# Cross-attention and FFN on one core: FFN products as 7 block products of half the size, and a new path for weights and products

## The reference

```python
x = x + attention(layernorm(x), ctx, ctx, Wq, Wk, Wv, Wo)      # 32 heads, 8 key/value heads
xn = layernorm(x)                                              # 1792 x 1024
g = xn @ (w1 * w1_scale).T                                     # w1: 3584 x 1024, one scale per 128x128 block
u = xn @ (w3 * w3_scale).T
h = silu(g) * u                                                # 1792 x 3584
out = x + h @ (w2 * w2_scale).T                                # w2: 1024 x 3584
```

## Time and profile before

| what | us |
|---|---|
| median of 3 runs | 2817.81 (2813.53 to 3363.06) |
| span of the profiled execution | 2817.7 |
| up to the end of attention | 897.8 |
| first output projection and norm | 897.8 to 997.0 |
| FFN, first half (with transposes) | 997.0 to 1890.5 |
| rest of it, second output projection | 1890.5 to 1996.5 |
| FFN, second half | 1996.5 to 2817.7 |

### The profile page before, as it was taken

How to read it: one execution, slowest core, us unless ns; L and a number is a source line. 1 busy time by engine, 2 the same in 40 slices (tenths; PEclk the granted TensorE clock), 3 DMA queues, 4 the chain that set the end, 5 groups by cost and what they waited for, 6 DMA issues and landing times. The chain is left out here.

```text
span 2817.7 us, 39477 instructions
## 1 busy us (share of the span) xinstructions
PE 2730.8 (97%) x14320; PEld 2311.9 (82%) x14320; DVE 1277.8 (45%) x2198; ACT 790.0 (28%) x1452; POOL 476.3 (17%) x221
## 2 busy tenths in 40 slices
PE   7989999999997999999999999999999999999999
PEld 6978777777763788888888888887888888888888
DVE  6425776777674533333333333335443333433343
ACT  3222444444444132222222222212211111112110
POOL 1000444444454121121111111100000000000000
PEclk9989999999986999999999999999999999999999
DMA  7525555454452332323222222243111111111101
GB/s 213 162 83 160 126 130 143 130 126 129 123 114 79 115 135 98 120 97 107 100 89 97 97 89 89 97 134 120 60 60 60 45 60 45 60 60 45 59 30 53
DMA packets 184786, 277.32 MB, mean 98 GB/s; under 512 B 62368, under 2 KB 140576, under 8 KB 184720
## 3 DMA queue, kind: packets, MB, share of 16 engines
q1 hardware_dynamic: 184720, 276.43, 32.0%
HBM read 190.20 MB, written 85.72 MB: 98 GB/s over the span
## 5 line engine op out<-in xcount | busy, mean ns | idle before, releaser
L74 PE MATMUL bank<-x_h,f_w_h 128*128 128x448 f32 x1792 | 667.3, 372 | 3.1 <-DVE f_w_l L80 3.1
L76 PE MATMUL bank<-x_h,f_w_l 128*128 128x448 f32 x1792 | 657.7, 367 | 0.0
L75 PE MATMUL bank<-x_l,f_w_h 128*128 128x448 f32 x1792 | 657.5, 367 | 0.0
L74 PEld LDWEIGHTS bank<-x_h,f_w_h 128*128 128x128 f32 x1792 | 337.6, 188 | 31.7 <-DVE f_w_l L80 3.5
L76 PEld LDWEIGHTS bank<-x_h,f_w_l 128*128 128x128 f32 x1792 | 337.3, 188 | 29.6
L75 PEld LDWEIGHTS bank<-x_l,f_w_h 128*128 128x128 f32 x1792 | 337.8, 189 | 28.4
L1341 DVE TENSOR_TENSOR f_hf<-bank,f_gate 128x448 f32<-128x448 f32 x112 | 69.6, 622 | 603.1 <-PE bank L76 524.8
L1353 DVE TENSOR_TENSOR y<-bank,y 128x512 f32<-128x512 f32 x392 | 270.1, 689 | 150.9 <-PE bank L76 148.2
L691 DVE TENSOR_REDUCE a_nm<-bank 112x1 f32<-112x375 f32 x512 | 268.1, 535 | 144.2 <-PE bank L826 141.5
L74 PE MATMUL bank<-f_w_h,f_h_h 128*128 128x512 f32 x784 | 312.4, 398 | 0.0
L76 PE MATMUL bank<-f_w_h,f_h_l 128*128 128x512 f32 x784 | 306.4, 391 | 0.0
(11 more groups left out here) (105 smaller groups left out, 3991.2 us busy)
## 6 DMA issues: line engine op xcount, KB each, us to landing
stash<-in_L_ffn_w SPq DMA_DIRECT2D x84, 512.0 KB, 4.6
weight_scratch<-f_wt SPq DMA_DIRECT2D x84, 512.0 KB, 2.7
stash<-weight_scratch SPq DMA_DIRECT2D x84, 512.0 KB, 4.0
stash<-in_ctx SPq DMA_DIRECT2D x48, 500.0 KB
a_qst<-q_scratch SPq DMA_DIRECT2D x96, 224.0 KB, 4.8
a_kst<-k_scratch SPq DMA_DIRECT2D x96, 188.0 KB, 4.2
stash<-in_L_xattn_Wo SPq DMA_DIRECT2D x64, 128.0 KB, 4.1
q_xn<-in_x SPq DMA_DIRECT2D x16, 448.0 KB, 6.0
```

What stands on the lines that cost most here:

```text
L74: pe.matmul(acc, lh, rh, start=first, stop=False)
L75: pe.matmul(acc, lh, rl, start=False, stop=False)
L76: return pe.matmul(acc, ll, rh, start=False, stop=last)
```

## The change

**Output projection.** `mixing()` runs once over all 14 tiles. Each tile with its residual goes to DRAM (`y_scratch`). The normalised tile is written with its columns in another order (32 columns of each of four quarters side by side) and transposed by PE; ACT alone copies the result, to `xT` for the first 7 tiles, and through `x_scratch` for the last 7. At its end SP waits for these stores.

**Gate and up products** (`gate_up`). The 1,792 tokens are two passes of 896 (g = 0, 1). A pass goes over 28 units `mi` (14 pairs of row chunks P, first w1 and then w3, m = 0 and 1). A unit is a 256x1024 block of weights by 1024x896 of tokens, as 2x2 blocks by 2x2 blocks in the Strassen-Winograd form: 7 block products i = 0 to 6, each 4 weight tiles (128x128) by 448 columns, 12 matmuls, 84 in a unit (before: 96). Their weight operands are three of the quarters and four sums S of them (POOL, `sums`), the token operands three blocks and four sums T. The products add up in three PSUM banks per parity of `mi` and in three tiles `su` on DVE (`add`, 5 per unit). h is stored to DRAM, as 3 blocks and 4 sums (POOL, `hidden_sums`), for the later down projection.

**Weights.** ACT multiplies the raw weights by their scales (`scale_raw`), DVE transposes them in blocks of 32x32 (`make_wT`, 4 passes per unit), SP stores them for the second pass (1 MB) and loads the raw weights of the unit after (1 MB, four DMAs to 32 partitions each, runs of 1 KB), into one buffer. In the second pass the transposed weights are read back, and the same is done with w2: `load_raw2` (1 MB, four DMAs to 32 partitions, runs of 256 bytes), `scale_raw2` (ACT, 8 passes of 128x256), `make_w2T` (DVE, 4 passes), `down_sums` (POOL, 4 passes), `store_w2`.

**Down projection** (`down`). After both passes, 7 block products of 896 x 1792 by 1792 x 512, each 7 tiles of 128 tokens, each 14 x 3 = 42 matmuls of 512 columns (49 x 42 = 2,058; before 2,352). Its operands are loaded from DRAM and split again. The residual (7.3 MB) is loaded at its start.

The PE transposes of weights are gone. The number of DMAs to 32 partitions and the waits that stand between them are new.

```diff
@@ gate_up, SP @@
+                        for mi in range(2 * NM):
+                            if mi == 2:
...
+                                sp.dma_start(xT[:, :, :], x_scr).then_inc(x_loaded_, 16)
+                            if mi >= NM + 2 and mi % 2 == 0:
+                                store_w2((mi - NM) // 2 - 1)
+                            if NM <= mi + 2 < 2 * NM:
+                                load_wT(mi + 2)
+                            if mi >= 2 and mi % 2 == 0:
+                                store_h(mi // 2 - 1)
+                            if mi + 2 < NM:
+                                store_wT(mi + 2)
+                                if mi + 3 < NM:
+                                    load_raw(sp, mi + 3)
+                            if mi >= NM and mi % 2 == 0:
+                                load_raw2((mi - NM) // 2)
+                        def store_wT(mi):
+                            sp.wait_ge(wT_made, 4 * mi + 4)
+                            sp.dma_start(wt_scr[mi], wT[:, mi % 2]).then_inc(wT_stored[mi % 2], 16)
+                        def store_h(P_):
...
+                            sp.wait_ge(h_done, 4 * P_ + 4)
+                            for i, b in ((0, H11), (2, H21), (5, H22)):
...
+                            for k, i in enumerate((4, 1, 3, 6)):
+                                sp.wait_ge(Sh_made, 4 * P_ + k + 1)
...
@@ gate_up, POOL: sums (S), hidden_sums, down_sums are 4 tensor_tensor each @@
+                        def sums(mi):
...
+                            wait_wT(pool, mi)
+                            wait(pool, w_lo, 7 * (mi - 1) + 5)
+                            pool.tensor_tensor(s1, a21, a22, ALU.add).then_inc(S_made, 1)
...
+                            wait(pool, w_lo, 7 * (mi - 1) + 7)
+                            pool.wait_ge(S_made, 4 * mi + 2)
+                            pool.tensor_tensor(s4, a12, s2, ALU.subtract).then_inc(S_made, 1)
+                        for mi in range(2 * NM):
+                            if mi >= 2 and mi % 2 == 0:
+                                hidden_sums(mi // 2 - 1)
...
+                            if mi + 2 < 2 * NM:
+                                sums(mi + 2)
+                            if mi > NM and mi % 2 == 1:
+                                down_sums((mi - NM) // 2)
@@ gate_up, ACT @@
+                        def first_copy(mi):
+                            P_ = mi // 2
+                            act.wait_ge(prod, 7 * mi + 1)
...
+                            nc.scalar.activation(su[:, 0, :], A_[mi % 2][:, 0:TB], ACT.Copy
+                                                 ).then_inc(first_out, 1)
+                            for i in range(7):
+                                act.wait_ge(prod, 7 * mi + i + 1)
+                                if i == 0:
+                                    first_copy(mi)
...
+                                        gate(P_, H11, A_[0][:, 0:TB])
+                                if mi == NM - 1:
+                                    split_x(1, i)
+                                if nxt:
+                                    split_w(mi + 1, i)
+                                if mi % 2 == 0:
+                                    if i in (4, 5, 6):
+                                        act.wait_ge(summed, 5 * mi + i - 1)
+                                        gate(P_, {4: H22, 5: H21, 6: H12}[i],
+                                             su[:, {4: 2, 5: 0, 6: 1}[i], :])
+                                if i == 1 and mi + 2 < NM:
+                                    scale_raw(mi + 2)
+                                if i == 3 and mi >= NM and mi % 2 == 0:
+                                    scale_raw2((mi - NM) // 2)
@@ gate_up, DVE @@
+                            for i in range(7):
+                                dve.wait_ge(prod, 7 * mi + i + 1)
+                                if i == 1:
...
+                                    add(mi, 1, B_, 0)
+                                elif i == 3:
+                                    add(mi, 2, B_, 0)
...
+                                if nxt:
+                                    split_w(mi + 1, i)
+                                if up and i >= 4:
...
+                                    hidden(P_, b, su[:, slot, :], i - 2)
+                                if 2 <= i <= 5 and mi + 2 < NM:
+                                    make_wT(mi + 2, i - 2)
+                                if i < 4 and mi >= NM and up:
+                                    make_w2T((mi - NM) // 2, i)
@@ gate_up, PE @@
+                                pe.wait_ge(w_lo, 7 * mi + i + 1)
...
+                                elif i == 2:
+                                    pe.wait_ge(first_out, mi + 1)
+                                elif i == 3:
+                                    pe.wait_ge(summed, 5 * mi + 1)
...
+                                elif i == 5:
+                                    pe.wait_ge(summed, 5 * mi + 2)
+                                elif i == 6:
+                                    pe.wait_ge(summed, 5 * mi + 3)
@@ down, SP @@
+                        sp.wait_ge(b_stored, 112 * NP)
+                        load_b(0, 0)
...
+                        load_a(0)
...
+                        load_b(0, 1)
+                        load_a(1)
...
+                        for t in range(MT):
+                            for r in range(2):
+                                for at, n, tok in rows(r, t):
+                                    sp.dma_start(y[at:at + n, r, t, :], y_scr[tok:tok + n, :]
+                                                 ).then_inc(y_loaded, 16)
...
+                        for n in range(N):
+                            i, t = n // MT, n % MT
+                            if n + 2 < N:
+                                load_a(n + 2)
```

More of the change, by code:

```diff
@@ L148, in load13 @@
[L148 to L162, removed]
-                src = wt_scr[bass.ds(2 * p + par, 1), 2].rearrange("a p n -> (a p) n")
-            sp.dma_start(dst, src).then_inc(r2_loaded[half][par], 16)
@@ L981, in _ @@
+                        store_xT(NT_TOK - 1)
+                        for s in range(2):
+                            sp.wait_ge(res_stored[s], 16 * NT_TOK // 2)
+                            sp.wait_ge(xT_stored[s], 16 * ((MT + s) // 2))
                     @block.gpsimd
                     def _(pool):
[L983 to L987 removed]
@@ L1114, in _ @@
                                     last.then_inc(o_done, 1)
-                        def step(t, slot, use):
-                            products(t, slot)
-                            transposes(t - 1, 1 - slot)
-                        tiles(pe, step)
-                        transposes(TT - 1, 0)
-        def ffn(half, y, x2_h, x2_l):
+                        for t in range(1, NT_TOK):
+                            products(t)
+                            transposes(t - 1)
+                        transposes(NT_TOK - 1)
@@ L1441, in pair @@
-                        def pair(p, more):
-                            for par in range(2):
-                                for tb in range(2):
-                                    gate_up(p, par, tb, more)
-                            pe.wait_ge(t_lo, t2_first(p, 1) + T2)
-                            for t in range(TT):
-                                down(p, t)
-                                if more and t < T13 and half == 0:
-                                    transpose13(p + 1, 1, t)
@@ L1458, in build_program @@
         queries()
         attention()
-        y = top.enter_context(nc.sbuf_tensor("y", [P, TT, D], f32))
-        x2_h = top.enter_context(nc.sbuf_tensor("x2_h", [P, KT, HALF], f32r))
-        x2_l = top.enter_context(nc.sbuf_tensor("x2_l", [P, KT, HALF], f32r))
-        for half in range(2):
-            mixing(half, y, x2_h, x2_l)
-            ffn(half, y, x2_h, x2_l)
+        with nc.sbuf_tensor("xT", [P, KT, HALF], f32) as xT:
+            mixing(xT)
+            gate_up(xT)
+        down()
```

1013 lines of the change are left out of this document (612 added, 401 removed).

## The result

The changed kernel takes 2944.66 us (median of 4 runs, 2941.84 to 2947.65). The kernel before took 2817.89 us beside it, so the ratio is 1.0456, with a 95% interval of 1.0441 to 1.0472: slower. (One of the four runs of the kernel before took 3363.06 us, in a slow state, and is left out of the ratio.) Forecast were 2859 us, 1.5% slower, and a difference that can't be told from none was the likeliest case. The time lies in the range, but the loss of 127 us is three times the forecast one and can be told from none.

The account below looks back on a forecast made before the run. PE's matmul count bound the old kernel; two waiting loops would bound the new one. First add 1126, first pass 547, change of passes 77.5, second pass 591, end of block 21, down 496: 2859 us, range 2700 to 2950.

Parts of the forecast that it names:

- A0: DVE's `add` at i = 3 of unit 0 in the first pass, forecast at about 1126 us.
- F0: PE's product 2 of the first up unit of the second pass, forecast at 1751 us.
- What bounds the kernel, and what PE would save: Whole kernel: PE's count of matmuls sets the time; some 240 us saved if nothing else became late.
- The first rival: Both passes: the followers keep up and PE stays the bound, 2587 us; chance 0.17 for one loop or both absent.
- both loops: Closed chains: first pass through the raw buffer, 21.9 us per unit; second through SP and POOL, 45.5 per pair; chance 0.45.
- First pass: Loop through the one raw buffer, PE's product 5 waiting for DVE's `add`: 21.9 us per unit against 17.0, 25 units.
- the rival of the slow transpose: First pass: DVE transpose at twice the split, 1.35 us, adds 70 us, 2930 in all; chance 0.13.
- Second pass: Loop through SP, POOL and raw w2, PE's product 2 waiting for ACT's first copy: 45.5 us per pair against 34.0.
- Short runs cost double: Second pass: raw w2's 256-byte runs add 6.3 us per pair for 13 pairs, 2942 us in all; chance 0.15.
- Change of passes: From unit 25's `add` at i = 3 to the second pass's first product 2: 77.5 us.
- Down: Down projection: PE starts 13.7 us in, goes on at 43 after two tiles, then 47 tiles take 447.5; 496 in all.
- The start: Start of gate and up: 47 us of PE waiting for the tokens' operands, from 1078.7 to about 1126.

Follow-up runs that it names:

- e6: Changed kernel with raw w2 loaded early, first-pass load ahead of the store, and DVE transposes two at i = 3 and two at i = 4: 2611.28 us, ratio 0.9278.
- e7: As e6, with the residual in `down` loaded tile by tile between operand loads: 2596.12 us, ratio 0.9235.
- e8: Changed kernel with raw w2 issued ahead of the seven stores of h, still after the last sum of h: 2894.62 us, ratio 1.0281.
- e2: Changed kernel with raw w2 read in runs of 8 KB instead of 256 bytes, same byte count: 2916.68 us, ratio 1.0358.
- e4: Changed kernel with first-pass load ahead of the store, and ACT's scaling and DVE's transposes one product later: 2848.73 us, ratio 1.0109.
- e1: Changed kernel with the load of raw w2 put ahead of the stores in SP's order: 2734.68 us, ratio 0.9701.

## Why the prediction was wrong, step by step

The waits that the prediction named are all in the profile after, with other sizes.

| term | forecast | measured | miss |
|---|---|---|---|
| first `add` at i = 3 (A0) | 1126 | 1113.9 | -12 |
| first pass, 25 units | 547 (21.9 each) | 560.6 (22.4) | +14 |
| change of passes to F0 | 77.5 | 90.2 | +13 |
| second pass, 13 pairs | 591 (45.5 each) | 651.4 (50.1) | +60 |
| to the start of `down` | 21 | 20.8 | 0 |
| `down` | 496 | 503.2 | +7 |
| end | 2859 | 2940.1 | +81 |

**What bounds the kernel, and what PE would save: right.** The first rival put the time without both loops at 2587. With the loops cut it was measured at 2611 (e6), and with the residual spread as well at 2596 (e7). So the Strassen products do bring some 220 us, and the changed kernel loses them and 127 more to order.

**First pass: right in mechanism and size.** The ring through the one raw buffer, with its waits and its 22.0 us in the steady stretch, is as forecast; the 14 us of the table lie at its ends, the first round taking 26.9 us and the last three about 23.1. Store and load were put at 9.8 us and took 10.1 from the load's side. The DVE transpose, the least certain price, was put at 0.65 and took 0.703 us for 128x512:

```profile
L1441 DVE STREAM_TRANSPOSE stash<-stash x112: 669/703/711, 1074.8 to 1681.4; 128x512 f32<-128x512 f32 x112
```

so the rival of the slow transpose falls.

**Second pass: the step that failed.** The links were right, and the term for the last store's issue and raw w2 (latency 2.6, data 6.3, with issues 9.3) was mis-sized: 12.4 was measured. I counted the load as if its queue were empty. But SP issues seven stores of h, 1.6 MB, within 4.5 us just ahead of it, and such a store takes 4.9 us from issue to landing, so that their data is still under way. e8 moved only this: without the stores in front the term is 8.6 us, 0.7 below the 9.3 I had forecast. So the miss of the term, 3.1 us, is 3.8 of queueing that I had put at nothing, less 0.7 that I had too much for the load itself. The miss makes 40 of the 60 us in 13 rounds, and e8 gave 50 back. I had taken such queueing into account twice elsewhere, for the store ahead of the first pass's load and for the residual ahead of the third tile's operand, and left it out here.

The other links missed by less, in both directions: PE's five products 14.9 instead of 13.65 (its slow start costs 2.5 and not 1.3; the first product takes 4.6 us), DVE's `add` and split 2.3 instead of 1.3 (POOL was in a pass), POOL 12.9 instead of 14.3, ACT 8.2 instead of 7.0, of which the eight scalings make 0.6 (3.3 for 2.7). In this pair they add up to some 2 us.

**Short runs cost double: refuted as sized.** The time came out at 2945, and this rival had said 2942. By the total alone it would have been declared right. e2 shows that it isn't: with runs of 8 KB a pair is 2.2 us shorter, where this rival had put 6.3 us on top. The 4,096 runs of 256 bytes cost about 2 us more than the same 1.05 MB in long runs, behind the stores of h in both cases. That is close to the 1.7 us between the prediction's 6.3 and its 4.6 at 226 GB/s: its own price was about right, and 2942 was met by luck. The Trainium skill (DMA: Bandwidth & Descriptors, Specifications) has transfers below 512 bytes done as read, modify, write, and puts no price on it there; this load into SBUF shows a surcharge, but no doubling of the 6.3 us.

**Change of passes: 13 us short.** POOL's three passes over 1792 columns for the second half's tokens fell together with DVE's splits of weights for the next unit. POOL:

```profile
1693.83 4.52 POOL L1296 TENSOR_TENSOR g_t<-xT 128x1792 f32<-128x1792 f32 x1
1698.43 4.39 POOL L1300 TENSOR_TENSOR stash<-xT,g_t 128x1792 f32<-128x1792 f32 x1
1702.78 4.51 POOL L1302 TENSOR_TENSOR xT<-xT 128x1792 f32<-128x1792 f32 x1
```

and DVE in the same stretch:

```profile
1695.18 3.72 DVE L90 TENSOR_TENSOR g_WL<-stash,g_WH 128x512 fp32r<-128x512 f32 x1
...
1699.36 4.02 DVE L90 TENSOR_TENSOR g_WL<-stash,g_WH 128x512 fp32r<-128x512 f32 x1
...
1703.83 4.00 DVE L90 TENSOR_TENSOR g_WL<-stash,g_WH 128x512 fp32r<-128x512 f32 x1
```

Each of the three splits ended about 0.55 us after a pass of POOL's did, and they took 3.7 to 4.0 us instead of 0.69: 9.7 us more. The mechanism stood in the text, "more with POOL's passes", without a number. That these 9.7 are the larger part of the 13 is read from the rows and wasn't tried by an experiment.

**Down: right but for the 7 us** by which the third tile's operand came later: the stall was put at 6.3 (43, less 13.7 for the start and 23 for two tiles) and took 14.0. e7 shows that it is the residual in front: with the residual spread no gap over 0.5 us is left in `down` behind its start.

**The start: 12 us too dear.** Gate and up begin at 1072.2 instead of 1078.7, and DVE's passes over 1792 columns took 2.0 where POOL was quiet.

**The chances.** Both loops "about as sized" had 0.45 and the range 2790 to 2910; the loops were there, and a size was off by a tenth. An error in a link is multiplied by the rounds: 1.2 us more per pair would already have led out of "no change", as the text itself worked out. With four links known to a microsecond at best, the range around the likeliest case was too narrow on the upper side, where unpriced queueing could only add. That 2945 lies inside the whole range, 2700 to 2950, is luck: its upper part was there for the two slow rivals, and neither of them came true.

## What to carry to other kernels

Where no engine is full and one waits a fixed time in each round, write down the ring that closes on itself and sum its links; a shorter link pays in every round, turning the ring (e4) pays nothing, and opening it (e1) pays most. A load that a ring waits for must be issued when its buffer comes free, ahead of stores that nobody waits for. When a load's time is worked out, add the bytes of whatever was issued just before it on the same queue; with 1.6 MB in front, 8.6 us from the last sum to the consumer became 12.4.

## What the hardware showed that I had not expected

- DVE's split of 128x512 with two inputs in SBUF waits out a whole pass of POOL: 0.69 us alone, 1.2 to 1.8 beside POOL's passes of 512 columns, 3.7 to 4.0 beside those of 1792. Its mean over the kernel is 995 ns. POOL's pass of 512 columns took 1.29 us alone and up to 1.75 beside DVE. With the ring open this cost nothing (e7's pairs take 33.97 us with the same contention).
- SP's issues of short runs go slowly behind other transfers: four loads of 1,024 runs took 6.7 us to issue behind the stores and 3.5 us without them; four of 32 long runs took 2.5 us behind the same stores (e2).
- After a gap of 14 us PE's first product of 12 matmuls took 4.6 us instead of 2.43, at a granted clock of 0.50. Over the second pass the clock was 0.85; with the gaps gone it is 0.99. The gap costs twice, once as idle time and once behind it.
